# Gate order, fills from SBUF, kept weights, and final sums by accumulating transfers in a graph and expert layer

## The chip, the cores and the metric

The kernel runs on one core of one Trainium2 chip. The metric is the time that the device takes for one execution, in microseconds (us). Before the change it is 1561.77 us, the median of three runs (1561.69, 1561.77, 1563.81).

## The reference

`x` has 10000 rows of 128 values, `adj` is 10000 x 10000. First comes a graph layer, then a layer of eight experts of which each row uses the best two:

```
def _L0_gnn_ref(user_feat, item_feat, adj, W_item, b_item, W_user, b_user):
    h = item_feat @ W_item.T + b_item
    b = user_feat @ W_user.T + b_user
    return relu(adj @ h + b)
x = x + _L0_gnn_ref(layernorm(x), item_feat, adj, ...)
# experts, on xf = layernorm(x): N = 10000, D = 128, H = 256, E = 8
probs = softmax(xf @ gate_w + gate_b)
top2_vals, top2_idx = top_k(probs, 2)
cw = zeros((N, E)).at[rows, top2_idx].add(top2_vals)
for e in range(E):
    acc += cw[:, e] * (gelu(xf @ W1[e] + b1[e]) @ W2[e] + b2[e])
x = x + acc
```

All values are float32. The kernel gets that precision from TensorE by splitting a float32 operand into a rounded part ("hi") and the remainder ("lo") and adding three products.

## The kernel before

**Graph stage.** The 10000 output rows are 20 blocks of 500 (`UB`). A block runs through 26 chunks (`CH`) of 384 rows of `adj`; the counter `n` goes over all 520 (`NCH`), and `c` is the chunk within its block. For each chunk SyncE loads 750 KB into one of six buffers (`load_raw`, L295), ScalarE rounds them into `a_hi` (L743, three buffers), the vector engine makes the remainder `a_lo` (L952, two buffers), and TensorE runs nine matmuls (L497, L498, L502). `load_raw(n)` waits until the remainder of chunk n - 6 is made.

**Gate work.** While block b runs, the finished block b - 1 is taken through layer norm, gate logits, softmax, the two best experts, a prefix count and the slots of its rows. Each piece stands at a chunk number of its own, the constants `X1_AT` to `TABLE_AT`: statistics at c = 4 and 5 (`stats2`, `stats1`), then eleven small Pool instructions for the inverse deviation (`rstd`, L1315 to L1331, issued at `BN1_AT`), which `logits` (L998, `LG_AT`) and `ln2_norm` on ScalarE (L788, `LN2_AT`) wait for, Pool's `power` (L1335), `softmax`, `top`, `mask`, `prefix`, `slots`. At `SLOT_AT` Pool sends every row of the block with eight indirect transfers (L1344) to its slots in the HBM tensor `zs`, twice, once for each chosen expert.

**Expert tiles.** The first 17 blocks (`S`) are served in this sparse way, in two groups (12 and 5 blocks). After a group's last block the vector engine makes a table of tiles of 512 rows (`table`). SyncE then fills the end of each expert's region from a spare region of `zs` (`fill_ends`, eight transfers from HBM to HBM, all at `n == FILL_AT[g]`), since the last tile of an expert is not full, and after the first fill loads weights and rows of tiles 0 and 1. There are 48 tiles (`NT`), spread over the chunks that are left by `W1_AT` and the lists made from it: tile rows loaded (`load_zt`), turned (L581), two expert layers, turned back, and sent by Pool with indirect transfers (L1353) to the HBM tensor `rr`, in the original row order, the first choice to its first half and the second choice to its second.

**Dense items.** The last three blocks are done densely: 24 items (`ND`, three blocks by eight experts), one per step d after chunk 520, on all engines. In a step ScalarE does the two gelus (L857), a rounding (`dense_round`) and a weight rounding (`w_round`); the vector engine does `scale` (L1174), `dense_rest` (L1178), `w_rest` (L1135) and `comb_add`; TensorE `dense_w1`, `dense_wbc`, `dense_w2`. The gate of the last block (p = 19) runs in the same steps: logits at d = 6, softmax at d = 10. Weights are loaded and split again for each of the 24 items.

**Final sums.** For each of the 17 sparse blocks SyncE loads three 256 KB pieces (the stored rows of `out_s` and the two halves of `rr`) into SBUF, three buffers of each (`CB`), the vector engine adds them (L1187 and L1189), and SyncE stores the sum. This runs in the steps of the dense items (`COMB_AT`).

Every engine takes its instructions in the written order and waits on semaphores. No planner is used; the order is made by the constants above.

## Time and profile before

| | |
|---|---|
| median of three runs | 1561.77 us |
| the profiled execution's own time | 1562.79 us |
| its span | 1561.0 us |
| granted TensorE clock, mean | 0.979 |
| busy: matmuls, vector engine, ScalarE, Pool | 1476.0, 1278.2, 1103.5, 807.3 us |
| moved | 502.29 MB, mean 322 GB/s |

The page divides the span into 40 slices of 39 us and gives the busy tenths of each engine in them:

```profile
PE   8999999999999999999996899999999989999887
DVE  5778788788788887887885788888888978788898
ACT  4666767667677677677673778797878768787655
POOL 0114534634635544446344178776877865676420
```

TensorE is busy in nearly all of them; slice 22 (around 850 us) and the last ones are lower. A busy share says nothing on what is late, so the rows below come from waits, timelines and windows.

### The profile page before, as it was taken

How to read it: one execution, taken by the hardware profiler on the slowest of the kernel's cores; microseconds unless marked ns; L12 is line 12 of the kernel's file. 1: busy time of each engine (PE TensorE's matmuls, PEld its weight loads, DVE VectorE, ACT ScalarE, POOL GpSimd, SP SyncE). 2: the span in 40 equal slices, each digit the busy share in tenths (PEclk: the TensorE clock that was granted, in tenths of full speed). 3: DMA queues.
4: the chain of work that ended last, by engine and by line, in shares of the span. 5: the costliest groups of instructions: out<-in, count | busy, mean ns of one | idle time of the engine just before them, and what ended most of it. 6: DMA issues, size and time to landing. Idle time of an engine off the chain costs nothing.

```text
span 1561.0 us, 20673 instructions
## 1 busy us (share of the span) xinstructions
PE 1476.0 (95%) x6682; PEld 1181.8 (76%) x6682; DVE 1278.2 (82%) x1677; ACT 1103.5 (71%) x1178; POOL 807.3 (52%) x596
## 2 busy tenths in 40 slices
PE   8999999999999999999996899999999989999887
PEld 6787787787787877877875688888888877777555
DVE  5778788788788887887885788888888978788898
ACT  4666767667677677677673778797878768787655
POOL 0114534634635544446344178776877865676420
PEclk9999999999999999999998899999999999999999
DMA  9889999999999999999996998989898888786675
GB/s 356 298 315 337 351 371 345 354 365 335 369 346 340 375 343 343 382 331 355 364 331 227 348 329 320 334 331 333 322 332 326 324 306 304 273 280 226 215 237 195
DMA packets 144649, 502.29 MB, mean 322 GB/s; under 512 B 35696, under 2 KB 41792, under 8 KB 144286
## 3 DMA queue, kind: packets, MB, share of 16 engines
q1 hardware_dynamic: 127518, 479.25, 84.1%
q0 software_dynamic: 17024, 21.73, 4.1%
q8 instruction: 53, 0.87, 0.2%
q14 instruction: 54, 0.44, 0.1%
HBM read 468.77 MB, written 36.31 MB: 324 GB/s over the span
## 4 chain that ended last, share of the span: by engine, by line
PE 57%; DVE 15%; POOL 13%; issue 7%; ACT 3%; DMA 3%; SPq 2%; DVEq 0%; ACTq 0%; POOLq 0%
PE p_agg L502 16%; PE p_agg L497 14%; PE p_agg L498 14%; DVE s_a_lo L952 6%; POOL s_rs L1315 3%; POOL rr L1353 2%; POOL s_rs L1327 2%; PE p_hid L479 2%; DVE s_h_hi L1178 1%; POOL s_rs L1316 1%; ACT s_a_hi L743 1%; DMA s_raw<-adj 1%; POOL s_rs L1319 1%; PE p_agg L513 1%; PE p_hid L590 1%
## 5 line engine op out<-in xcount | busy, mean ns | idle before, releaser
L952 DVE TENSOR_TENSOR s_a_lo<-s_raw,s_a_hi 128x1500 fp32r<-128x1500 f32 x520 | 885.6, 1717 | 144.7 <-PE p_agg L502 92.4
L743 ACT ACTIVATE s_a_hi<-s_raw 128x1500 fp32r<-128x1500 f32 x520 | 751.0, 1454 | 220.2 <-PE p_agg L502 183.1
L497 PE MATMUL p_agg<-s_a_hi,s_h_hi 128*128 128x500 f32 x1560 | 635.4, 407 | 22.7 <-ACT s_a_hi L743 22.7
L498 PE MATMUL p_agg<-s_a_hi,s_h_lo 128*128 128x500 f32 x1560 | 615.1, 394 | 0.0
L502 PE MATMUL p_agg<-s_a_lo,s_h_hi 128*128 128x500 f32 x1560 | 450.8, 398 | 33.4 <-DVE s_a_lo L952 31.8
L1344 POOL DMA_INDIRECT zs<-s_rows,s_idx x136 | 225.6, 1659 | 309.2 <-DVE s_idx L1080 215.3
L502 PEld LDWEIGHTS p_agg<-s_a_lo,s_h_hi 128*128 128x128 f32 x1560 | 293.9, 191 | 115.1 <-DVE s_a_lo L952 56.6
L497 PEld LDWEIGHTS p_agg<-s_a_hi,s_h_hi 128*128 128x128 f32 x1560 | 299.4, 192 | 87.6 <-ACT s_a_hi L743 29.4
L498 PEld LDWEIGHTS p_agg<-s_a_hi,s_h_lo 128*128 128x128 f32 x1560 | 299.8, 192 | 58.1 <-issue 3.2
L1353 POOL DMA_INDIRECT rr<-s_ysb,s_dests x192 | 271.7, 1415 | 136.7 <-DVE s_ysb L1163 84.4
L1335 POOL TENSOR_TENSOR s_gt<-s_ebase,s_gt 125x32 f32<-125x32 f32 x20 | 129.9, 6495 | 48.3 <-DVE s_gt L1006 48.1
L1315 POOL TENSOR_TENSOR s_rs<-s_bn 125x8 f32<-125x8 f32 (+1 forms) x21 | 42.0, 2002 | 146.3 <-DVE s_bn L971 135.5
L1154 DVE TENSOR_TENSOR s_gl<-s_g,s_gh 128x1024 fp32r<-128x1024 f32 x48 | 58.8, 1226 | 57.1 <-ACT s_gh L833 57.1
L826 ACT ACTIVATE s_g<-p_hid,s_bias 128x512 f32<-128x512 f32 x96 | 60.5, 683 | 41.0 <-PE p_hid L592 41.0
L833 ACT ACTIVATE s_gh<-s_g 128x1024 fp32r<-128x1024 f32 x48 | 51.0, 1062 | 16.1 <-PE p_y L608 15.0
L788 ACT ACTIVATE s_rows<-p_agg,s_rs 125x128 f32<-125x128 f32 x80 | 29.9, 454 | 42.6 <-POOL s_rs L1331 42.6
L839 ACT ACTIVATE s_yt<-p_y,s_bias 128x512 f32<-128x512 f32 x48 | 32.8, 683 | 30.3 <-PE p_y L608 30.3
L590 PE MATMUL p_hid<-s_zh,s_wt 128*128 128x512 f32 (+1 forms) x106 | 43.2, 408 | 0.4 <-ACT s_g L857 0.4
L819 ACT ACTIVATE s_zh<-p_tp 128x512 fp32r<-128x512 f32 x48 | 28.0, 584 | 20.1 <-PE p_hid L592 18.1
L591 PE MATMUL p_hid<-s_zh,s_wt 128*128 128x512 f32 (+1 forms) x106 | 41.6, 392 | 0.0
L592 PE MATMUL p_hid<-s_zl,s_wt 128*128 128x512 f32 (+1 forms) x106 | 41.6, 392 | 0.0
L1135 DVE TENSOR_TENSOR s_wt<-s_wraw,s_wt 128x512 fp32r<-128x512 f32 x60 | 40.8, 680 | 0.0
(215 smaller groups left out, 1433.2 us busy)
## 6 DMA issues: line engine op xcount, KB each, us to landing
s_raw<-adj SPq DMA_DIRECT2D x520, 750.0 KB, 6.7
s_wraw<-w SPq DMA_DIRECT2D x72, 256.0 KB, 4.1
s_zt<-zs SPq DMA_DIRECT2D x48, 264.0 KB, 3.1
s_raw<-rr SPq DMA_DIRECT2D x34, 256.0 KB, 3.8
s_xtok<-x_tok SPq DMA_DIRECT2D x20, 256.0 KB, 6.8
s_xt<-x_t SPq DMA_DIRECT2D x20, 250.0 KB, 7.1
out_s<-s_x1s SPq DMA_DIRECT2D x17, 256.0 KB, 6.9
s_raw<-out_s SPq DMA_DIRECT2D x17, 256.0 KB, 3.3
```

The lines of the kernel that those rows point to most:

```text
L497: mm(o, h_hi[:, k * D:(k + 1) * D], hi, start=(k == 0), stop=False)
L498: mm(o, h_lo[:, k * D:(k + 1) * D], hi, start=False, stop=False)
L502: last = mm(o, h_hi[:, k * D:(k + 1) * D], a_lo[:, n % LOS, j * UB:(j + 1) * UB], start=False, stop=False)
L590: mm(hid[h][:, 0:n], w_hi, hi, start=True, stop=False)
L743: fn(a_hi[:, n % HIS, :], raw[:, n % RAW, :], ACT.Copy).then_inc(hi_made, 1)
L826: fn(g[:, h * T:(h + 1) * T], hid[h][:, :], ACT.Gelu, bias=bias[:, k % 4, h:h + 1])\
L952: tt(a_lo[:, n % LOS, :], raw[:, n % RAW, :], a_hi[:, n % HIS, :].bitcast(F32), ALU.subtract)\
L1154: tt(gl[:, :], g[:, :], gh[:, :].bitcast(F32), ALU.subtract).then_inc(gl_made, 1)
L1315: tt(row[0], even, odd, ALU.add)
L1335: gp.tensor_tensor(gt[0:TS, 2, :], ebase[0:TS, :], gt[0:TS, 1, :], ALU.pow).then_inc(ez_made, 1)
L1344: gp.indirect_dma_start(out=zs[:, :], out_offset=bass.IndirectOffsetOnAxis(ap=idx[0:TS, j:j + 1].bitcast(U32), axis=0), in_=rows[k][0:TS, ...
L1353: gp.indirect_dma_start(out=rr[:, :], out_offset=bass.IndirectOffsetOnAxis(ap=dests[:, k % XR, s:s + 1].bitcast(U32), axis=0), in_=yrows(k ...
```

## The change

```diff
-X1_AT, X1T_AT, BN2_AT, BN1_AT, X1S_AT, LG_AT, LN2_AT = 1, 1, 4, 5, 4, 9, 10
-TAILHI_AT, TAILLO_AT, SOFT_AT, TOP1_AT, TOP2_AT, LN1_AT = 9, 10, 15, 16, 17, 13
-PREFIX_AT, LN1T_AT, SLOT_AT, LN1C_AT = 18, 16, 20, 19
-TABLE_AT = (20, 21, 22)
+X1_AT, X1T_AT, BN2_AT, BN1_AT, X1S_AT, LG_AT, LN2_AT = 1, 1, 4, 5, 4, 11, 12
+TAILHI_AT, TAILLO_AT, SOFT_AT, TOP1_AT, TOP2_AT, LN1_AT = 9, 10, 16, 17, 18, 15
+PREFIX_AT, LN1T_AT, SLOT_AT, LN1C_AT = 19, 17, 21, 20
+TABLE_AT = (21, 22, 23)
...
-CB = 3
-FILL_AT = [(hi + 1) * CH + 5 for lo, hi in GROUPS]
-FIRST_W1 = [(hi + 1) * CH + 10 for lo, hi in GROUPS]
+CB = 12
+FILL_AT = [(hi + 1) * CH + 6 for lo, hi in GROUPS]
+FIRST_W1 = [at + E // 2 + 4 for at in FILL_AT]
...
-ZT_LOAD = [0, 0] + [max(W1_AT[k - 2] + 3, FILL_AT[k >= NTG[0]] + 1) for k in range(2, NT)]
-COMB_AT = [p + p // CB for p in range(S)]
+ZT_LOAD = [0, 0] + [max(W1_AT[k - 2] + 3, FILL_AT[k >= NTG[0]] + E // 2) for k in range(2, NT)]
+COMB_AT = [p if p < GROUPS[1][0] else p + 3 for p in range(S)]
+COMB_OUT = [6 + p if p < GROUPS[1][0] else p + 10 for p in range(S)]
...
+            def fill_end(g, e):
+                if e == 0:
+                    sp.wait_ge(scattered, 2 * 16 * SUBS * GROUPS[g][1])
+                    sp.wait_ge(tab_made, 2 * (g + 1))
+                r = sp.value_load(fillat[0:1, g, e:e + 1], min_val=0, max_val=SPARE0[g] - T)
+                sp.dma_start(zs[bass.ds(r, T), :].rearrange("(p s) w -> p (s w)", s=SUBS),
+                             fill.rearrange("p s w -> p (s w)")).then_inc(filled, 16)
...
-                    if n == FILL_AT[g_]:
-                        fill_ends(g_)
-                if n == FILL_AT[0] + 1:
+                    if 0 <= n - FILL_AT[g_] < E // 2:
+                        fill_end(g_, 2 * (n - FILL_AT[g_]))
+                        fill_end(g_, 2 * (n - FILL_AT[g_]) + 1)
+                if n == FILL_AT[0] + E // 2:
                     load_w(0)
...
-                if j + 4 < ND:
+                if j + 4 < E:
                     load_w(NT + j + 4)
...
+            def comb_add(p, k):            # on Pool
+                ...
+                pool.wait_ge(comb_loaded[p % CB], 16 * (p // CB + 1))
+                if k == 1:
+                    pool.wait_ge(comb_added[p % CB], 32 * (p // CB) + 16)
+                row = k * RANK + p * T
+                gp.dma_start(comb(p), rr[row:row + T, :].rearrange("(p s) d -> p (s d)", s=SUBS), accum_op=ALU.add)\
+                    .then_inc(comb_added[p % CB], 16)
...
-                        if k == NT - 2:
-                            power(BLOCKS - 1)
+            for first, last in ((0, GROUPS[1][0]), (GROUPS[1][0], S)):
+                for p in range(first, last + 2):
+                    if p < last:
+                        comb_add(p, 0)
+                    if p - 2 >= first:
+                        comb_add(p - 2, 1)
+                    if p == 4:
+                        power(BLOCKS - 1)
```

It has four parts. The gate pieces stand one or two chunks later. The fills are written from an SBUF tile (`fill`, in the space of the early constants) two at a time over four chunks, from `FILL_AT` on, and the first tiles' loads come after the last of them; the tiles keep their chunks. In the dense steps the eight experts' weights stay in SBUF (three sets where they were, five in the space of `h_lo`), so 8 loads and splits are left of 24; all biases come once, early, in `dbias`. And the final sums are made by 34 transfers that Pool issues and that add a piece of `rr` onto the loaded rows of `out_s` in SBUF; there are 12 buffers, the stores stand in the dense steps by `COMB_OUT`, and the power of the last block's gate stands among the adds, after the eighth. The vector engine's `comb_add` is gone.

## Rows read from the trace of the kernel before

**Rows 1.** Waits, TensorE 100 to 830, then 0 to 830, then whole: us, times, longest.
```profile
PE p_agg L502 <- DVE s_a_lo L952: 28.2, 14, 2.3
DVE s_gt L998 <- POOL s_rs L1331: 39.5, 12, 3.3
ACT s_a_hi L743 <- DMA s_raw<-adj: 36.2, 9, 17.9
```
**Rows 2.** Timeline of Pool at 720 us: start, duration, instruction, idle before.
```profile
720.87 3.24 POOL L1315 TENSOR_TENSOR s_rs<-s_bn 125x8 f32<-125x8 f32 x1 [9.24 <-DVE s_bn L971]
...
728.67 1.67 POOL L1327 TENSOR_TENSOR s_rs<-s_rs,s_consts 125x8 f32<-125x8 f32 x1
...
730.70 0.20 POOL L1331 TENSOR_TENSOR s_rs<-s_rs,s_consts 125x8 f32<-125x8 f32 x1
```
**Rows 3.** Timeline of the vector engine and TensorE at the same place.
```profile
726.05 1.76 DVE L952 TENSOR_TENSOR s_a_lo<-s_raw,s_a_hi 128x1500 fp32r<-128x1500 f32 x1 [0.32 <-PE p_agg L502]
731.01 0.19 DVE L998 TENSOR_TENSOR s_gt<-p_small,s_rs 125x32 f32<-125x32 f32 x1 [3.19 <-POOL s_rs L1331]
...
731.79 1.71 DVE L952 TENSOR_TENSOR s_a_lo<-s_raw,s_a_hi 128x1500 fp32r<-128x1500 f32 x1
...
733.55 0.94 PE L502 MATMUL p_agg<-s_a_lo,s_h_hi 128*128 128x500 f32 x3 [2.18 <-DVE s_a_lo L952]
```
**Rows 4.** Chain in order of time, 720 to 745: start, us, what.
```profile
735.28 0.42 PE p_agg L498
...
739.22 0.23 PE p_agg L497
```
**Rows 5.** Windows: stretch, its us, busy (count) by engine, clock, DMA share, GB/s.
```profile
513.00:574.00 61.00, 58.42 (x266) 47.31 (x265) 50.89 (x62) 43.20 (x39) 30.40 (x21) 1.00 0.96 354
```
**Rows 6.** First fill: SyncE's wait, its fills, TensorE's first matmul after.
```profile
SPq L380 <- DMA zs<-s_rows,s_idx: 11.6, 1, 11.6
...
842.37 10.22 SPq L381 DMA_DIRECT2D zs<-zs  x8
...
860.64 0.78 PE L497 MATMUL p_agg<-s_a_hi,s_h_hi 128*128 128x500 f32 x1 [14.88 <-ACT s_a_hi L743]
```
**Rows 7.** Timeline: turn of tile 0, and TensorE after the second fill.
```profile
871.32 0.60 PE L581 MATMUL p_tp<-s_ident,s_zt 128*128 128x128 f32 x4
...
1273.27 0.49 PE L497 MATMUL p_agg<-s_a_hi,s_h_hi 128*128 128x500 f32 x1 [3.82 <-ACT s_a_hi L743]
```
**Rows 8.** Groups by line and shape, 1451 to 1561: busy us, mean ns, idle before.
```profile
L1178 DVE TENSOR_TENSOR s_h_hi<-s_raw,s_h_hi 128x1000 fp32r<-128x1000 f32 x12 | 14.3, 1193 | 0.0
...
L1189 DVE TENSOR_TENSOR s_raw<-s_raw 128x512 f32<-128x512 f32 x17 | 11.8, 692 | 0.6
...
L1135 DVE TENSOR_TENSOR s_h_hi<-s_wraw,s_h_hi 128x512 fp32r<-128x512 f32 x12 | 8.2, 682 | 0.0
```
**Rows 9.** Timeline: the first scale of the dense items, and the last two.
```profile
1453.94 1.19 DVE L1174 TENSOR_TENSOR s_raw<-s_raw,p_agg 128x1000 f32<-128x1000 f32 x1
...
1547.63 1.20 DVE L1174 TENSOR_TENSOR s_raw<-s_raw,p_y 128x1000 f32<-128x1000 f32 x1 [0.77 <-ACT s_raw L857]
...
1551.31 1.20 DVE L1174 TENSOR_TENSOR s_g<-s_g,p_y 128x1000 f32<-128x1000 f32 x1
```
**Rows 10.** Timeline: a small Pool sum started behind an L952 at 1104.40.
```profile
1104.43 1.75 POOL L1325 TENSOR_TENSOR s_rs<-s_rs 125x8 f32<-125x8 f32 x1
```
**Rows 11.** Timeline of Pool's last instructions.
```profile
1482.74 5.46 POOL L1335 TENSOR_TENSOR s_gt<-s_ebase,s_gt 125x32 f32<-125x32 f32 x1 [9.78 <-DVE s_gt L1006]
1488.40 1.52 POOL L1353 DMA_INDIRECT rr<-s_ysb,s_dests  x1 [0.20 <-issue]
1490.23 0.96 POOL L1353 DMA_INDIRECT rr<-s_ysb,s_dests  x1 [0.30 <-issue]
```
**Rows 12.** DMA issues with KB and median us to landing; chain, 1380 to 1450.
```profile
s_raw<-rr SPq DMA_DIRECT2D x34, 256.0 KB, 3.8
...
1401.41 5.79 DMA rr<-s_ysb,s_dests
```

More of the change, by code:

```diff
@@ L140, in build @@
         dests = sb("dests", [P, XR, SUBS], I32)
-        early = sb("early", [P, 3 * D])
+        early = sb("early", [P, SUBS * W])
         wi, ones, bbs = early[:, 0:D], early[:, D:2 * D], early[0:4, 2 * D:3 * D]
@@ L159, in build @@
         ints = sb("ints", [1, NTHR + NTG[0] + E * E])
-        fill = ysb[:, :, :].rearrange("p a n -> p (a n)")[:, 0:SUBS * W].rearrange("p (s w) -> p s w", w=W)
+        fill = early[:, :].rearrange("p (s w) -> p s w", w=W)
         bn = sb("bn", [P, 2 * SUBS, 6])
@@ L225, in build @@
         sent = [sem("sent0"), sem("sent1")]
-        rr_zeroed, comb_mid, comb_made = sem("rr_zeroed"), sem("comb_mid"), sem("comb_made")
+        rr_zeroed = sem("rr_zeroed")
+        comb_added = [sem(f"comb_added{i}") for i in range(CB)]
         comb_loaded = [sem(f"comb_loaded{i}") for i in range(CB)]
@@ L265, in wpart, with comb, parts_made @@
         def wpart(o, lo):
-            i = (o - NT) % 6
-            if o >= NT and i >= 3:
-                w0 = 12 * UB + (i - 3) * 4 * HID + lo * 2 * HID
-                return h_hi[:, w0:w0 + 2 * HID]
+            e = (o - NT) % E
+            if o >= NT and e >= 3:
+                w0 = (e - 3) * 4 * HID + lo * 2 * HID
+                return h_lo[:, w0:w0 + 2 * HID]
+            if o >= NT:
+                return wt[:, e, lo, :]
             return wt[:, o % 3, lo, :]
-        def wpart_before(o):
-            return o - 3 if o < NT + 3 else o - 6
         def yrows(k):
             return ysb[:, k % 2, :]
-        def comb(p, i):
-            c0 = 2 * UB + p % CB * 3 * T + i * T
+        def comb(p):
+            c0 = 2 * UB + p % CB * T
             return flat[:, c0:c0 + T]
-        def tiles_to(o):
-            return min(o, NT)
+        def parts_made(o):
+            return min(o, NT + E - 1) + 1
         block = ctx.enter_context(nc.Block())
@@ L446, in _ @@
             load_w(NT + 3)
-            for j in range(ND + 4):
+            for j in range(ND + 5):
                 for p in range(S):
-                    if COMB_AT[p] == j - 3:
+                    if COMB_OUT[p] == j:
                         comb_store(p)
@@ L804, in w_round @@
             def w_round(o):
-                act.wait_ge(w_loaded[o % 2], 32 * (o // 2 + 1))
-                before = wpart_before(o)
-                if NT + 3 <= o < NT + 6:
+                late = max(o - NT + 2, 0) // 2
+                act.wait_ge(w_loaded[o % 2], 32 * (o // 2 + 1) - 16 * late)
+                if o >= NT + 3:
                     act.wait_ge(chunk_used, NCH)
-                elif before >= 0:
-                    act.wait_ge(w2_done, before + 1)
+                elif o >= 3:
+                    act.wait_ge(w2_done, o - 2)
                 fn(wpart(o, 0), wraw[:, o % 2, :], ACT.Copy).then_inc(w_hi, 1)
@@ L932, in _ @@
                     dense_round(d - 1)
-                if d >= 0 and d + 2 < ND:
+                if 0 <= d and d + 2 < E:
                     w_round(NT + d + 2)
@@ L1272, in _ @@
                     dense_rest(d - 1)
-                if d >= 0 and d + 2 < ND:
+                if 0 <= d and d + 2 < E:
                     w_rest(NT + d + 2)
-                for p in range(S):
-                    if COMB_AT[p] == d - 2:
-                        comb_add(p)
                 if d >= E + 3 and (d - 3) % E == 0:
@@ L1335, in power @@
                 gp.tensor_tensor(gt[0:TS, 2, :], ebase[0:TS, :], gt[0:TS, 1, :], ALU.pow).then_inc(ez_made, 1)
+            def comb_add(p, k):
+                if k == 0 and p == 0:
+                    pool.wait_ge(rr_zeroed, 16 * 3)
+                if k == 0 and (p == 0 or p == GROUPS[1][0]):
+                    for i in range(2):
+                        pool.wait_ge(sent[i], 16 * SUBS * tiles_of(i, NT if p else NTG[0]))
+                pool.wait_ge(comb_loaded[p % CB], 16 * (p // CB + 1))
[4 more added lines that the diff above has]
+                    .then_inc(comb_added[p % CB], 16)
             def scatter(p):
@@ L1363, in _ @@
             gp.memset(rows[1][:, :, :], 0.0).then_inc(sets, 1)
-            gp.memset(ysb[:, :, :], 0.0).then_inc(sets, 1)
-            pool.wait_ge(sets, 5)
+            pool.wait_ge(sets, 4)
             pool.wait_ge(late_loaded, 16 * NL)
-            gp.tensor_scalar(fill[:, :, D + 1], dest0[:, :], float(DUMP + 2 * T), None, ALU.add).then_inc(spare_set, 1)
             for i in range(2):
@@ L1383, in _ @@
                         scatter(p)
+                if n == 2 * CH:
+                    pool.wait_ge(h_prod, CH + 1)
+                    pool.wait_ge(gsum_done, 1)
+                    pool.wait_ge(bb_split, 1)
+                    gp.memset(fill, 0.0).then_inc(fill_set, 1)
+                    pool.wait_ge(fill_set, 1)
+                    gp.tensor_scalar(fill[:, :, D + 1], dest0[:, :], float(DUMP + 2 * T), None, ALU.add)\
+                        .then_inc(fill_set, 1)
                 for k in range(NT):
```

67 lines of the change are left out of this document (25 added, 42 removed).

## The prediction

> **What bounds the kernel now.** I read the table of waits first, then one block of the graph stage in the timeline, then the two fills, then the dense stage. In the first half TensorE is the limit: between 100 and 830 us its matmuls stood still only 28.2 us, all of it behind the remainder chunks of L952 [rows 1]. The block at 720 us shows where this comes from. The eleven small Pool instructions of `rstd` begin at 720.87 and the last one at 730.70; the vector engine reaches `logits` (L998) at 727.8 and idles 3.19 us for them [rows 2, 3]. The next remainder starts at 731.79 in place of 728.10 (one chunk of 2.05 us behind 726.05), 3.69 us late, and the matmuls lose 2.18 us: so TensorE has 1.5 us of slack there. After the idle time its matmuls come 0.42 us apart (granted clock low), then 0.23 us again [rows 4]. Ten of them at the lower level cost 2.0 us. The waits count 12 such blocks; one stretch of a block (513 to 574) shows full clock, so not each of them pays the 2.0 us [rows 1, 5].
>
> The second loss is the fill at 842 us. SyncE waited 11.6 us for the last scatter, then issued eight HBM-to-HBM fills in 10.22 us, and raw chunks stood behind all that; TensorE idled 14.88 us, restarted at the low clock, and reached the first expert tile's turn (L581) only at 871.32 [rows 6, 7]. The second fill cost 3.82 us of idle and some slow matmuls [rows 7].
>
> The third is the end. From 1452 us on, one dense item of the vector engine is scale 1.19, remainder 1.19, weight remainder 0.68 and, for 17 items, two sums of 0.69 [rows 8]; from the first scale at 1453.94 to the last at 1551.31 that is 97.4 us for 23 steps, 4.23 each. The step from 1547.63 to 1551.31 has no weight remainder, and its two sums fit beside ScalarE: 3.68 us, set by the ring scale, remainder, gelu [rows 9].
>
> **The change part by part.** All is summed against the profiled execution, 1562.79 us, of which the span is 1561.0.
>
> *Gate order.* `logits` moves two chunks later (9 to 11), `ln2_norm` to 12, the rest of the gate mostly by one. Two chunks are 4.1 us, more than the 3.2 us wait, so on paper the wait goes. The rows speak against the whole of it: a small Pool sum takes 0.20 us, but 1.75 us when an L952 started just before it [rows 2, 10]. At 727.9 us six Pool instructions are left. With the vector engine idle they take 3.0 us. In the new order it runs two more remainders and `tail_rest` in that time, gaps of 0.3 us at most, so Pool gets through perhaps two of the six; the power (1.67) and the two behind it come after 732.1, where `logits` now stands waiting. I get `rs` at 734.4, the next remainder at 735.2, 3.1 us late against 3.69 before: TensorE waits 1.5 us and not 2.2. Over 12 blocks 0.65 x 12 = 7.8 us. An idle time of 1.5 us may no longer drop the clock each time; I take four drops fewer, 4 x 2.0 = 8.0 us. Sum 15.8. Ends: no drop saved and 0.3 us a block, 4 us; the stall gone with its slow matmuls, 12 x 4.2 = 50 us. I stay near the low end because a wait of 3.0 us of Pool's own work can't shrink while its engine neighbour is busy. Raw chunks needed faster have room: ScalarE waited for raw data in nine places only, 36.2 us in all, 17.9 of it in one at the first fill [rows 1]. Behind the later waits of softmax and `slots` stand five chunks in place of six for a Pool power of 5.5 us or more [rows 11]; five are 10 us or more, so I cost this at 0.
>
> *Fills.* Scatter and fill both move one chunk, so the 11.6 us wait stays. Then two fills (2.6 us at 1.28 each, from SBUF) come before a raw chunk, where eight (10.2) did. The ring holds one chunk more, so TensorE runs dry at 848, and raw 345 lands near 851.5: idle 5 us in place of 14.9. But the loads of tile 0 now stand behind all fills and four raw chunks, near 861, and TensorE is in order: it waits for that tile at chunk 345 until about 864.6, and is slow again. The turn of tile 0 comes 6.7 us earlier less 2 us of clock: gain 4.5 us (0 if a wait in the fills piles up, 12 if neither stands). For the second fill the raw chunk is in time; gain 4 of the 5.6 us lost (0 to 5.6). Sum 8.5.
>
> *Kept weights.* 16 of 24 weight loads, roundings (ScalarE) and remainders (0.68 us on the vector engine) go, and the biases come in one early load of many tiny rows behind which nothing was late: 0.
>
> *Sums by accumulating transfers.* All 34 sums leave the vector engine. With the weights gone a step is 3.68 us, bound by the ring: 3.32 + 22 x 3.68 = 84.3, plus 2.0 for the extra work at steps 11 and 14, against 97.4: 11.1 us. The new cost is in Pool's queue. `power` for the last block (5.46 us, now begun at 1482.74 right after `logits`, before the last send [rows 11]) moves behind the last send and eight accumulating transfers. An indirect send costs Pool 0.96 to 1.52 and 0.30 between [rows 11]; I take 1.45 for an add. The last send ends at 1478; three adds, a wait of 2 us for the first to land, five adds: 1491.5; power done at 1497.2. Softmax at step 10 would run at 1493.3, and behind it in the vector queue stand the scale and remainder of step 11, for which ScalarE and TensorE wait: 3.9 us, of which 3.6 are not covered, and a 0.5 us clock loss. Net gain 7.0. If an add costs 1.25, 9; if 2.7, softmax waits 12 us and the stage loses 1.
>
> The other 26 adds last until 1535; refilling a buffer before the second group costs 5, landing and store 9: 1549, five before the main path's end at 1554. The trace has no accumulating transfer. The nearest rows: a plain 256 KB load of `rr` lands in 3.8 us, an indirect send in 5.79 [rows 12]. By the order of issue two adds are in flight, so one per 1.45 us (Pool's issue) at best and one per 2.9 us if each takes 5.8: 34 x 2.9 = 99 us. I take the issue-bound value, since a plain load lands sooner than that. Stores wait on SyncE in order, and later loads of `out_s` stand behind them; the four items between hide that while adds land within about 6 us.
>
> Pool's sends take 0.96 to 1.52 us beside a busy vector engine [rows 11]. The Trainium skill ("SBUF — State Buffer", the box on the vector engine blocking DMA) warns that transfers issued by GpSimd starve while that engine holds the shared port, and gives some 3.1 us in place of 0.62 for one; by it 34 adds would take 105 us and the tail would end after that of before. The trace does not agree for these sends; no run shows it for an accumulating one.
>
> **Sum.** 15.8 + 8.5 + 0 + 7.0 = 31.3; 1562.8 - 31.3 = 1531.5; the median of the runs shown is 1.0 below the profiled one: 1531.
>
> **Rivals.** *A, the gate wait is gone wholly*: the two chunks suffice and 50 us come back in place of 15.8. For it: 4.1 > 3.2 and no idle, no clock loss. Against it: [rows 10]. Time 1497. *B, the gate stall keeps its clock falls and the fills merely move*: 4 + 4 + 7 = 15; 1547. For it: 1.5 us of idle is much still. *C, the adds become the bound, the slower side*: Pool's accumulating transfers land in 5.8 us or more, one per 2.9 us; they begin at 1478, so the last is done at 1577, with the refill, landing and store 1590, 29 us past the old end, and 24.3 us of gate and fills don't cover it: 1566. It decides from 2.7 us per add on, where the tail's loss equals those 24. For it: each reads and writes SBUF besides reading HBM; against it the 3.8 us landing [rows 12]. *D, the change hits a wait that I don't see in the expert stage* (power one chunk closer to softmax behind Pool's sends), 48 tiles losing 0.5 us each: 1555.
>
> **How the numbers follow.** Forecast 0.45, A 0.15, B 0.2, C 0.12, D 0.08. 1531 is the likeliest. Its own range is 1518 to 1545 (gate 8 to 24, fills 3 to 13, tail -1 to 9). The range over cases goes down into A and up to just short of C: 1502 to 1561. A measurement of this kernel tells 0.2% (3 us). Faster: forecast, A, B and most of D, 0.85; slower: C less its mild half, and some of D, 0.11; same 0.04.
>
> **What would show it.** Right: at `logits` in a first-half block the vector engine idles 2.2 to 2.5 us and L502 waits about 1.5; a Pool sum of 1.7 us stands between 728 and 732 of such a block; TensorE's idle at the first fill is two pieces of 5 and 8 us, the second ended by the `zt` load; dense steps of 3.68 us, one of 7 to 8 at softmax. Wrong: no idle before L998 at all (A); Pool's adds 2.5 us or more apart with the last store far behind the last dense output (C); waits on `ez` in the expert stage (D).

## The result and the profile after

The changed kernel takes 1535.07 us (median of 4 runs, 1534.02 to 1538.60) against 1562.79 for the kernel before (4 runs, 1561.69 to 1564.05), ratio 0.9829 with a 95% interval of 0.9817 to 0.9841: 27.7 us faster. The prediction was 1531, range 1502 to 1561. The profiled execution took 1538.60, span 1536.8, so the traces differ by 24.2 us only, and the changed kernel's other runs lie about 3.5 below its profiled one.

Where the 24.2 us come from is read by following one instruction through both traces. The remainder L952 runs once per chunk, 520 times; the start of number n in the trace of before less its start in the trace of after is what has been gained by then:

```
chunk number          4    28   104   312   338   346   366   370   390   468   480   519   end
gained by then, us  -3.8  -3.7  -1.2   4.3   4.7  17.6  15.0   9.1   8.5   8.8  15.9  16.0  24.2
```

So 3.8 us are lost at the very start, 8.6 gained in the graph stage, 10.2 at the first fill (338 to 366), 6.5 lost right behind it, 7.1 gained at the second fill (468 to 480), and 8.2 in the dense stage and the end.

*The gate.* The wait table of the changed kernel, 100 to 830 us (us in total, times, longest), answers to [rows 1]:

```profile
DVE s_gt L998 <- POOL s_rs L1320: 26.3, 12, 2.2
PE p_agg L501 <- DVE s_a_lo L952: 23.4, 22, 1.9
```

The vector engine idles 2.2 us for `rstd` where it idled 3.2, and TensorE's wait falls by only 4.8 us in all. At `logits` it falls from 2.2 or 2.3 to 1.6 in eleven of the twelve blocks (1.9 in one), 7.7 us together. But smaller waits have come behind it: 0.13 us where ScalarE is late after `ln2_norm`, and 0.3 us eight chunks later, beside the vector engine's `top`. The same block in the timelines, which answers to [rows 2, 3]:

```profile
717.04 3.23 POOL L1304 TENSOR_TENSOR s_rs<-s_bn 125x8 f32<-125x8 f32 x1 [7.64 <-DVE s_bn L971]
...
726.80 3.15 POOL L1316 TENSOR_TENSOR s_rs<-s_rs,s_consts 125x8 f32<-125x8 f32 x1
...
730.30 0.20 POOL L1320 TENSOR_TENSOR s_rs<-s_rs,s_consts 125x8 f32<-125x8 f32 x1
...
730.60 0.19 DVE L998 TENSOR_TENSOR s_gt<-p_small,s_rs 125x32 f32<-125x32 f32 x1 [2.20 <-POOL s_rs L1320]
...
734.08 3.35 DVE L952 TENSOR_TENSOR s_a_lo<-s_raw,s_a_hi 128x1500 fp32r<-128x1500 f32 x2 [0.98 <-ACT s_a_hi L742]
...
733.16 0.94 PE L501 MATMUL p_agg<-s_a_lo,s_h_hi 128*128 128x500 f32 x3 [1.58 <-DVE s_a_lo L952]
```

Pool's eleven instructions take 13.46 us from 717.04 to their end (13.2 to 13.5 in all twelve blocks); in [rows 2] they took 10.03. There the last six of them started after 727.9, when the vector engine was idle already; here only the last two did. What a block of 26 chunks costs is in the windows (stretch, its us, busy (count) of TensorE, its weight loads, vector engine, ScalarE and Pool, granted clock, DMA share, GB/s). First two blocks of the kernel before, one at full clock and one not:

```profile
507.20:567.60 60.40, 58.09 (x265) 47.09 (x264) 50.68 (x63) 42.62 (x39) 29.96 (x20) 1.00 0.95 349
628.40:689.40 61.00, 58.72 (x262) 48.04 (x262) 50.72 (x63) 42.66 (x38) 30.61 (x20) 0.97 0.97 362
```

and two of the changed one:

```profile
624.80:684.90 60.10, 57.98 (x264) 46.69 (x263) 50.68 (x63) 42.55 (x38) 33.57 (x20) 1.00 0.97 361
684.90:745.60 60.70, 58.74 (x260) 47.47 (x258) 50.81 (x62) 42.67 (x38) 33.22 (x20) 0.97 0.96 358
```

A fall of the clock costs a block 0.6 us, not 2.0, and the shorter stall saves it 0.3, not 0.65. Before, 11 of the 12 stretches from chunk 18 to 330 show 0.97 or 0.98; after, 4 do.

*The start.* SyncE and TensorE (the first line is the new load of all biases):

```profile
9.32 0.39 SPq L398 DMA_DIRECT2D s_dbias<-b  x1
9.75 3.77 SPq L399 DMA_DIRECT2D s_yt<-tri  x1
...
19.75 0.43 PE L475 MATMUL p_hid<-s_bbp,s_bselr 4*128 4x384 f32 x1 [1.63 <-DMA s_g<-feat_t]
```

The small load behind the biases held SyncE 3.77 us (0.33 in the kernel before), and raw and feature chunks stood behind it.

*The fills*, answering to [rows 6, 7]. In the kernel before, TensorE had a second idle time behind the 14.88 us, and on SyncE the loads of tiles 0 and 1 stood between the first raw chunk behind the fills and the second:

```profile
852.64 0.57 SPq L295 DMA_DIRECT2D s_raw<-adj  x1
...
858.81 0.91 SPq L295 DMA_DIRECT2D s_raw<-adj  x2
...
867.74 0.79 PE L497 MATMUL p_agg<-s_a_hi,s_h_hi 128*128 128x500 f32 x1 [3.23 <-ACT s_a_hi L743]
```

In the changed kernel: SyncE's first two fills, TensorE's two idle times, and the turn of tile 0.

```profile
838.73 1.49 SPq L379 DMA_DIRECT2D zs<-s_early  x2
...
848.36 0.79 PE L496 MATMUL p_agg<-s_a_hi,s_h_hi 128*128 128x500 f32 x1 [5.71 <-ACT s_a_hi L742]
...
865.19 0.78 PE L496 MATMUL p_agg<-s_a_hi,s_h_hi 128*128 128x500 f32 x1 [3.36 <-ACT s_a_hi L742]
...
868.65 0.60 PE L580 MATMUL p_tp<-s_ident,s_zt 128*128 128x128 f32 x4
```

The idle times fall from 18.1 us together to 9.1. Then comes a wait that the kernel before did not have. Pool issues the scatters of block 12 ahead of the send of tile 0, and tile 2's result has to wait for that send:

```profile
896.85 1.27 POOL L1346 DMA_INDIRECT zs<-s_rows,s_idx  x1 [22.27 <-DVE s_idx L1080]
...
917.70 0.99 POOL L1355 DMA_INDIRECT rr<-s_ysb,s_dests  x1 [0.30 <-issue]
...
927.93 0.69 DVE L1161 TENSOR_TENSOR s_ysb<-p_y,s_probs 128x512 f32<-128x512 f32 x1 [5.80 <-DMA rr<-s_ysb,s_dests]
...
930.91 1.62 PE L501 MATMUL p_agg<-s_a_lo,s_h_hi 128*128 128x500 f32 x3 [4.00 <-DVE s_a_lo L952]
```

At the second fill TensorE no longer idles at all ([rows 7] had 3.82).

*The end*, answering to [rows 9, 11]: first and last scale, softmax without a wait, Pool's power, the last vector result, the last accumulating transfer.

```profile
1437.72 1.19 DVE L1172 TENSOR_TENSOR s_raw<-s_raw,p_agg 128x1000 f32<-128x1000 f32 x1
...
1477.11 0.18 DVE L1013 TENSOR_REDUCE s_col<-s_gt 125x4 f32<-125x32 f32 x1
...
1522.53 1.20 DVE L1172 TENSOR_TENSOR s_g<-s_g,p_y 128x1000 f32<-128x1000 f32 x1 [1.38 <-ACT s_g L857]
...
1527.91 0.68 DVE L1181 TENSOR_TENSOR s_xt<-p_y,s_xt 128x500 f32<-128x500 f32 x1 [1.88 <-PE p_y L664]
...
1470.09 6.27 POOL L1324 TENSOR_TENSOR s_gt<-s_ebase,s_gt 125x32 f32<-125x32 f32 x1
...
1528.82 0.86 POOL L1336 DMA_DIRECT2D s_raw<-rr  x1 [2.53 <-DMA s_raw<-rr]
```

23 steps take 84.81 us (97.4 in [rows 9]); but for the first (3.15) and two of 3.95 and 4.03 they are 3.67 to 3.73 each. Yet the last accumulating transfer is issued after the last vector result, and the span ends 8.2 us behind that result (1536.8 less 1528.6), where it ended 2.5 behind it in the kernel before (last result 1557.76 to 1558.44). The adds on the page (busy us, mean ns, idle before; then KB and us to landing), and Pool's waits for them in the wait table of 1440 to 1537:

```profile
L1336 POOL DMA_DIRECT2D s_raw<-rr x34 | 31.0, 1134 | 32.8 <-DMA s_raw<-out_s 16.7
...
s_raw<-rr POOLq DMA_DIRECT2D x34, 256.0 KB, 6.7
```

```profile
POOL s_raw L1336 <- DMA s_raw<-out_s: 16.7, 5, 6.5
POOL s_raw L1336 <- DMA s_raw<-rr: 15.5, 9, 2.6
```

### The profile page after: what moved, and what is told of

Read it like the earlier page. It is cut to its first block, busy times and chain, and to the rows that moved or that the text cites. A ratio compares the mean times of both kernels' runs of the same rounds, so it can differ in the third digit from the quotient of the medians.

```text
span 1536.8 us, 20551 instructions
## 1 busy us (share of the span) xinstructions
PE 1469.6 (96%) x6682; PEld 1172.5 (76%) x6682; DVE 1248.4 (81%) x1627; ACT 1095.3 (71%) x1162; POOL 885.7 (58%) x630
## 4 chain that ended last, share of the span: by engine, by line
PE 49%; DVE 15%; POOL 14%; issue 8%; ACT 7%; DMA 5%; SPq 2%; POOLq 0%; ACTq 0%; DVEq 0%
PE p_agg L501 13%; PE p_agg L496 11%; PE p_agg L497 11%; DVE s_a_lo L952 9%; ACT s_a_hi L742 4%; POOL s_rs L1316 3%; DMA s_raw<-rr 3%; POOL s_rs L1304 2%; POOL zs L1346 2%; POOL s_rs L1312 1%; POOL s_rs L1305 1%; PE p_hid L478 1%; PE p_hid L589 1%; PE p_hid L591 1%; PE p_hid L590 1%
## 5 line engine op out<-in xcount | busy, mean ns | idle before, releaser
L952 DVE TENSOR_TENSOR s_a_lo<-s_raw,s_a_hi 128x1500 fp32r<-128x1500 f32 x520 | 885.8, 1718 | 139.4 <-PE p_agg L501 84.4
L496 PE MATMUL p_agg<-s_a_hi,s_h_hi 128*128 128x500 f32 x1560 | 630.6, 404 | 10.2 <-ACT s_a_hi L742 10.1
L1346 POOL DMA_INDIRECT zs<-s_rows,s_idx x136 | 231.9, 1705 | 306.3 <-DVE s_idx L1080 211.8
L501 PEld LDWEIGHTS p_agg<-s_a_lo,s_h_hi 128*128 128x128 f32 x1560 | 290.2, 190 | 120.2 <-DVE s_a_lo L952 63.3
L497 PEld LDWEIGHTS p_agg<-s_a_hi,s_h_lo 128*128 128x128 f32 x1560 | 297.3, 191 | 57.9 <-issue 3.2
L1355 POOL DMA_INDIRECT rr<-s_ysb,s_dests x192 | 277.4, 1445 | 102.7 <-issue 53.1
L1316 POOL TENSOR_TENSOR s_rs<-s_rs,s_consts 125x8 f32<-125x8 f32 (+1 forms) x21 | 55.7, 2655 | 1.6
L1336 POOL DMA_DIRECT2D s_raw<-rr x34 | 31.0, 1134 | 32.8 <-DMA s_raw<-out_s 16.7
L746 ACT ACTIVATE s_h_hi<-p_hid 128x384 fp32r<-128x384 f32 x26 | 12.8, 491 | 41.2 <-PE p_hid L478 41.2
L589 PE MATMUL p_hid<-s_zh,s_wt 128*128 128x512 f32 (+1 forms) x102 | 41.7, 409 | 0.4 <-ACT s_g L857 0.4
```

The lines of the kernel that those rows point to most:

```text
L496: mm(o, h_hi[:, k * D:(k + 1) * D], hi, start=(k == 0), stop=False)
L497: mm(o, h_lo[:, k * D:(k + 1) * D], hi, start=False, stop=False)
L501: last = mm(o, h_hi[:, k * D:(k + 1) * D], a_lo[:, n % LOS, j * UB:(j + 1) * UB], start=False, stop=False)
L952: tt(a_lo[:, n % LOS, :], raw[:, n % RAW, :], a_hi[:, n % HIS, :].bitcast(F32), ALU.subtract)\
L1316: tt(row[1], row[5], mhalf, ALU.pow).then_inc(rs_step, 1)
L1346: gp.indirect_dma_start(out=zs[:, :], out_offset=bass.IndirectOffsetOnAxis(ap=idx[0:TS, j:j + 1].bitcast(U32), axis=0), in_=rows[k][0:TS, ...
```

## The experiments

All are the changed kernel with the edit shown, but for the fourth; times are medians of 4 runs, ratios to the kernel before on the same chip, with 95% intervals. They ran on two chips, where the kernel before took 1561.74 to 1563.74 us, so a difference to the changed kernel's 1535.07 of 2 us or less says little. The "gained by" numbers are made as in the table above.

**Bias load later.**
```
-                    sp.dma_start(dbias[:, :, :], b12.rearrange("e p n -> p e n")).then_inc(late_loaded, 16)
...
+                if n == 40:
+                    sp.dma_start(dbias[:, :, :], b12.rearrange("e p n -> p e n")).then_inc(dbias_loaded, 16)
```


> The changed kernel with one edit: the one load of all biases (dbias) is issued at chunk 40 of the graph stage and not among the first small loads. Theory 'the bias load is paid': in the changed kernel's trace SyncE's next load (tri) takes 3.77 us behind it where it took 0.33, raw and feature chunks stand behind that, and the remainder of chunk 4 is 3.8 us late against the kernel before. Then that time comes back: the remainder of chunk 4 at 24.1 to 24.5 us and not 27.9, and about 3.8 us of the total, 1531.3. Rival 'the start has slack, what is lost there comes back in the first block': the total stays at 1535 within 1 us, and the lag against before is gone by chunk 52 anyway (it was 2.8 there, and 1.2 at chunk 104). A third: at chunk 40 the same many tiny rows hold up SyncE for 3.4 us again, and raw chunks with it; then less than 3.8 comes back, though six raw chunks are in the ring.

1536.67 us, ratio 0.9828 (0.9804 to 0.9852): no gain. In its trace the hold is gone and with it the lag at chunk 4, 0.5 us and not 3.8:

```profile
8.30 0.33 SPq L399 DMA_DIRECT2D s_yt<-tri  x1
```

The hold is the bias load's: it stands in all seven other traces with the early load (2.86 to 3.59 us) and in none without. At chunk 40 the next load is held too, as the third theory has it (its issue takes 1.38 us in place of 0.33), but no engine waits for it. The rival that the first block takes the lag back falls: this trace is 3.3 us ahead of the changed kernel's at chunk 4 and still 2.9 at chunk 519. What the hold costs is not settled all the same: the lags at chunk 4 in the seven other traces with the early load are 0.4 to 4.4 us (2.4 in the mean of all eight), and one without the hold was 2.0 late too (0.3 in the mean of six). The total shows no gain, and its interval is nearly 4 us wide to either side.

**Send first.**
```
-                    if c == SLOT_AT and p < S:
+                    if c == SLOT_AT and p < S and p != GROUPS[1][0]:
                         scatter(p)
...
                         send(k)
+                        if k == 0:
+                            scatter(GROUPS[1][0])
```


> The changed kernel with one edit: on Pool the eight scatters of block 12 (the first ones after the first fill) are issued behind the send of expert tile 0 and not ahead of it. Theory 'sends are queued behind the scatters': in the changed kernel's trace the vector engine waits 5.80 us at 922 for the send of tile 0, whose four transfers were issued at 917.7 behind scatters that began at 896.85; the matmuls L501 wait 4.00 us for it and run slowly after. Then the wait goes, TensorE has no idle of 4 us between 905 and 940, and 6 to 6.5 us come back: 1529. Rival 'Pool is simply full there': eight scatters and two sends take 22 us whatever their order, so the wait moves to the next tile (tile 3 waits for the send of tile 1) and less than 2 us come back: 1533 to 1535.

1530.83 us, ratio 0.9805 (0.9779 to 0.9832). Pool now sends first:

```profile
894.56 1.24 POOL L1355 DMA_INDIRECT rr<-s_ysb,s_dests  x1 [23.61 <-DVE s_ysb L1161]
...
901.03 1.21 POOL L1346 DMA_INDIRECT zs<-s_rows,s_idx  x1 [0.30 <-issue]
```

and from 905 to 935 no engine waits for a send. The gain at chunk 366 is still there at 370 (18.5 and 18.5; 15.0 and 9.1 in the changed kernel). The wait came from the order on Pool, and it cost 6 us at that place. The medians differ by 4.2, but the intervals of the two ratios overlap, so it is the trace that shows it. The rival, that Pool is full in either order, falls.

**Sums ahead.**
```
-COMB_AT = [p if p < GROUPS[1][0] else p + 3 for p in range(S)]
-COMB_OUT = [6 + p if p < GROUPS[1][0] else p + 10 for p in range(S)]
+COMB_AT = [p // 2 if p < CB else p - 5 for p in range(S)]
+COMB_OUT = [6 + p if p < GROUPS[1][0] else p + 8 for p in range(S)]
...
-                    if p - 2 >= first:
-                        comb_add(p - 2, 1)
+                    if p - 3 >= first:
+                        comb_add(p - 3, 1)
```


> The changed kernel with the order of the final sums changed: the loads of out_s into the twelve buffers are issued two per step from the start of the dense stage, and the second accumulating transfer of a piece comes three pieces behind its first, not two. Theory 'the adds end last': in the changed kernel's trace the last vector result is ready at 1528.6 and the end is at 1536.8, 8.2 us later, where it was 3.3 us after the last result in the kernel before; Pool waits 16.7 us for loads of out_s and 15.5 us for its own first transfers. Then the adds end before the last result and 4 to 5 us come back: 1530.5. Rival 'the adds are bound by transfers': each needs its 6.7 us landing and the queue lets few be in flight, so Pool's waits move and the end stays within 1.5 us: 1535. A second rival: more adds at once slow the last expert sends or dense steps (3.68 us a step): then steps grow.

1530.88 us, ratio 0.9793 (0.9774 to 0.9811). From chunk 519 to the end it gains 13.6 us over the kernel before, the changed one 8.2. The last add now stands ahead of the last vector result, and the span (1530.0) ends 2.8 us behind that (timeline, and Pool's wait in the wait table of 1440 to 1531):

```profile
1520.50 0.86 POOL L1336 DMA_DIRECT2D s_raw<-rr  x1 [3.05 <-DMA s_raw<-rr]
...
1526.56 0.68 DVE L1181 TENSOR_TENSOR s_xt<-p_y,s_xt 128x500 f32<-128x500 f32 x1 [1.87 <-PE p_y L664]
```

```profile
POOL s_raw L1336 <- DMA s_raw<-rr: 25.0, 11, 6.4
```

The steps stay at 3.68. The waits for loads are gone, those for Pool's own transfers grew from 15.5 to 25.0: the adds are bound by their landing now (8.7 us in the median, 6.7 in the changed kernel), but end in time.

**Gate order alone**, on the kernel before (first fill and first tile one chunk later with the scatter).
```
-X1_AT, X1T_AT, BN2_AT, BN1_AT, X1S_AT, LG_AT, LN2_AT = 1, 1, 4, 5, 4, 9, 10
...
+X1_AT, X1T_AT, BN2_AT, BN1_AT, X1S_AT, LG_AT, LN2_AT = 1, 1, 4, 5, 4, 11, 12
...
+FILL_AT = [(hi + 1) * CH + 6 for lo, hi in GROUPS]
+FIRST_W1 = [(hi + 1) * CH + 11 for lo, hi in GROUPS]
```


> The kernel before with the gate order of the changed one alone (logits 11, ln2_norm 12, softmax 16 and the rest by one or two; first fill and first expert tile one chunk later with the scatter). The prediction gave this part 15.8 us: 1547. Reading the two traces block by block gives less: a block of 26 chunks takes 61.2 us where the clock falls and 60.4 where not in the kernel before, 60.7 and 60.1 in the changed one, so 12 x 0.35 for the stall plus about 7 falls fewer x 0.8 = 9.5 us: 1554. If the stall had gone with its slow matmuls (rival A) it would be 1512.

1551.75 us, ratio 0.9936 (0.992 to 0.9953): 10.0 us, where the prediction has 15.8 and the reading of the traces 9.5. In its trace 8.5 us of that come between chunk 4 and 338, as in the changed kernel, and four of the twelve blocks show the low clock. Its second fill still idles:

```profile
1264.69 0.78 PE L497 MATMUL p_agg<-s_a_hi,s_h_hi 128*128 128x500 f32 x1 [3.89 <-ACT s_a_hi L743]
```

**Logits at 13.**
```
-X1_AT, X1T_AT, BN2_AT, BN1_AT, X1S_AT, LG_AT, LN2_AT = 1, 1, 4, 5, 4, 11, 12
...
+X1_AT, X1T_AT, BN2_AT, BN1_AT, X1S_AT, LG_AT, LN2_AT = 1, 1, 4, 5, 4, 13, 14
+TAILHI_AT, TAILLO_AT, SOFT_AT, TOP1_AT, TOP2_AT, LN1_AT = 9, 10, 17, 18, 19, 16
+PREFIX_AT, LN1T_AT, SLOT_AT, LN1C_AT = 20, 18, 22, 21
...
+FILL_AT = [(hi + 1) * CH + 7 for lo, hi in GROUPS]
```


> The changed kernel with logits two chunks later again (13, ln2_norm 14, softmax 17, slots 22, first fill and first tile one chunk later). Theory 'Pool's small instructions end only when the vector engine pauses': each remainder of L952 holds up one of them, so two more chunks (4.1 us) let about two more of the eleven through, the idle time before logits falls from 2.2 by about 1.0 as from 9 to 11 (3.19 to 2.20), and TensorE waits about 0.6 us a block where it waited 1.9: 12 to 14 us, 1522. Rival 'it is only time': 4.1 us more is over the 2.2 us wait, no idle at all before logits, the block at full clock takes 58.2 us (TensorE's busy time) and 22 to 26 us come back: 1511. Rival 'softmax now stands too close behind the power': four chunks are 8.2 us against a power of 6.8; then a wait on Pool stands before softmax and nothing comes back: 1535.

1517.06 us, ratio 0.9714 (0.9698 to 0.973): 18 us below the changed kernel, between the first theory's 1522 and the rival's 1511. The trace decides for the rival. Pool and the vector engine in the timeline, TensorE's waits from 100 to 790 us, and the window of one block:

```profile
691.85 3.24 POOL L1304 TENSOR_TENSOR s_rs<-s_bn 125x8 f32<-125x8 f32 x1 [5.59 <-DVE s_bn L971]
...
705.12 0.20 POOL L1320 TENSOR_TENSOR s_rs<-s_rs,s_consts 125x8 f32<-125x8 f32 x1
...
706.82 0.18 DVE L998 TENSOR_TENSOR s_gt<-p_small,s_rs 125x32 f32<-125x32 f32 x1
```

```profile
PE p_agg L501 <- DVE s_a_lo L952: 5.4, 18, 0.5
```

```profile
659.00:717.00 58.00, 57.33 (x262) 46.81 (x261) 50.74 (x63) 42.54 (x39) 33.19 (x20) 1.00 0.99 368
```

In this block Pool's chain again takes 13.47 us, with the vector engine at work to its end. Its length is no constant: over the twelve blocks it is 9.2 to 15.1 us here. But logits, now 15.0 us behind the chain's start, finds `rs` ready in all of them (its idle time is 0.2 us at most), the block takes 58 us at full clock, and between chunk 4 and 338 34.6 us are gained over the kernel before. The softmax rival costs nothing in this stage.

**Logits at 15.**
```
+X1_AT, X1T_AT, BN2_AT, BN1_AT, X1S_AT, LG_AT, LN2_AT = 1, 1, 4, 5, 4, 15, 16
+TAILHI_AT, TAILLO_AT, SOFT_AT, TOP1_AT, TOP2_AT, LN1_AT = 9, 10, 19, 20, 21, 18
+PREFIX_AT, LN1T_AT, SLOT_AT, LN1C_AT = 22, 20, 24, 22
+TABLE_AT = (24, 25, 26)
...
+FILL_AT = [(hi + 1) * CH + 9 for lo, hi in GROUPS]
```


> The same at 15 (ln2_norm 16, softmax 19, slots 24, first fill and first tile three chunks later than in the changed kernel). By the first theory the idle time before logits is 0.2 us or none now, TensorE waits nothing for the rest of the gate and a block takes 58.2 to 58.6 us; by the second it is as at 13 in the graph stage. Both fills and the expert stage come three chunks later, which leaves 6 us less to the expert tiles: in the graph stage 20 to 24 us come back, of the total 16 to 24: 1511 to 1519.

1538.10 us, ratio 0.9843 (0.9826 to 0.9859), a miss. The graph stage is as at 13 (57.8 to 57.9 us a block from the fifth on), 29.5 us gained at chunk 338. The expert stage loses it: 18.6 at 442 and 9.2 at 519. (The profiled execution was the longest of the four, 8.2 us above the median.) Starting the expert tiles three chunks later costs far more than 6 us. Among the longer waits are some for Pool's sends: the vector engine idles 7.4 us for one at 916 and 3.1 at 1024. Which of the waits the total pays for was not tested.

**Vector sums.** Three loads and two sums of the vector engine for each piece, `power` ahead of the last send, as in the kernel before; kept weights stay.
```
+                tt(comb(p, 1), comb(p, 1), comb(p, 2), ALU.add).then_inc(comb_mid, 1)
...
+                tt(comb(p, 0), comb(p, 0), comb(p, 1), ALU.add).then_inc(comb_made, 1)
...
-                gp.dma_start(comb(p), rr[row:row + T, :].rearrange("(p s) d -> p (s d)", s=SUBS), accum_op=ALU.add)\
-                    .then_inc(comb_added[p % CB], 16)
```


> The changed kernel with the final sums as before (three loads and two sums of the vector engine for each piece, power before the last send), kept weights and all else left as changed. Theory 'the steps come from the kept weights, the transfers only cost': the kernel before already took 3.68 us for the one step that had two sums and no weight remainder, so the steps stay at 3.68 to 3.8, the last vector result comes by 1530 and the end 3.3 us behind it and not 8.2: 1531 to 1533, faster than the changed kernel. Rival 'the transfers bring the steps down': with 1.2 us of sums back on the vector engine 17 steps take 4.2 and the end comes 8 us later: 1543.

1538.31 us, ratio 0.9848 (0.9831 to 0.9864), 3.2 above the changed kernel, which the two intervals just fail to separate. Both theories hold half. The end (1539.4) comes 2.7 us behind the last vector result (1536.66), much as in the kernel before (2.5), but that result comes 8.1 us later than in the changed kernel. Steps with sums alone do take 3.68; most of those that have a weight remainder or gate work beside the sums take 4.1 to 5.4, such as this one of 4.15 between two starts of the remainder:

```profile
1445.06 1.19 DVE L1180 TENSOR_TENSOR s_h_hi<-s_g,s_h_hi 128x1000 fp32r<-128x1000 f32 x1
...
1449.21 1.21 DVE L1180 TENSOR_TENSOR s_h_hi<-s_raw,s_h_hi 128x1000 fp32r<-128x1000 f32 x1
```

So the transfers give 8 us up to the last result and take 5.5 back behind it. This kernel also prices the kept weights: its dense stage differs from that of before in them (and in the biases that are loaded early) alone, and from chunk 519 to the end it gains 5.0 us over the kernel before. Against the kernel with the sums ahead the vector sums cost 7.4 us.

**Fills from HBM, fills in a row.**
```
# the first kernel
-                             fill.rearrange("p s w -> p (s w)")).then_inc(filled, 16)
+                             zs[SPARE0[g]:SPARE0[g] + T, :].rearrange("(p s) w -> p (s w)", s=SUBS)).then_inc(filled, 16)
# the second kernel
-                    if 0 <= n - FILL_AT[g_] < E // 2:
-                        fill_end(g_, 2 * (n - FILL_AT[g_]))
-                        fill_end(g_, 2 * (n - FILL_AT[g_]) + 1)
+                    if n == FILL_AT[g_]:
+                        for e in range(E):
+                            fill_end(g_, e)
```


> The changed kernel with the end-of-list fills read again from the spare rows in HBM, but still two before each of four raw chunks. In the changed kernel two fills from SBUF take SyncE 1.46 us and in the kernel before eight from HBM took 10.2 (2.6 for two). Theory 'the order gives the gain, the source adds a little': 1.1 us more before each raw chunk, 4.4 us more before the first expert tile's loads; the first fill's two idle times (5.71 and 3.36) grow by 1 to 4 us together, the second fill stays without an idle time: 1.5 to 5 us slower, 1537 to 1540. Rival 'the source gives the gain' (the HBM fills also slow the raw chunks that land beside them): the second fill gets back its 3.8 us of idle time and slow matmuls, the first up to 6: 1543 or more.

> The changed kernel with all eight fills from SBUF issued in a row ahead of the first raw chunk (as the kernel before did from HBM). 8 x 0.73 = 5.9 us of SyncE before that chunk where it was 1.5, so the first idle time of TensorE at the first fill grows from 5.7 to about 10, while the raw chunks behind come without fills between them and the second idle time of 3.4 goes; the first expert tile is loaded as early or earlier. Theory 'the fills' SyncE time is what the first stretch pays, in whatever order': the total stays within 2 us, 1534 to 1537. Rival 'the order gives the gain': 4 to 8 us slower, the second fill with an idle time again: 1540.

1538.40 us (ratio 0.9841, 0.9819 to 0.9863) and 1536.93 (0.9832, 0.9813 to 0.985): neither can be told from the changed kernel. SyncE and TensorE with the eight in a row:

```profile
837.43 8.76 SPq L379 DMA_DIRECT2D zs<-s_early  x8
...
852.69 0.78 PE L496 MATMUL p_agg<-s_a_hi,s_h_hi 128*128 128x500 f32 x1 [11.32 <-ACT s_a_hi L742]
```

The idle time is one of 11.3 us (TensorE's next is 0.58, at 864.33) and not two of 9.1 together, but from chunk 338 to 366 this kernel gains 9.9 us and the changed one 10.2. (Eight fills took 8.76 us and not 5.9: the 0.73 of the expectation is half the span of a pair, but the next fill starts 1.1 us behind the one before it, in a pair as in a row.) With the fills from HBM the idle times are 12.2 us together, within the 1 to 4 us more that were expected, and the gain is 9.1. Both kernels keep the gain at the second fill (7.2 and 7.4 us from chunk 468 to 480), where the gate order alone did not have it.

So neither the source nor the spreading is needed alone. What is left is the third part of the edit: the first tiles' loads stand four chunks behind the start of the fills and not one, and the first layer of the first tile eight and not five. For the first fill SyncE's queue speaks for it: in the kernel before, two raw chunks are 6.2 us apart there, with the tiles' loads between them (852.64 and 858.81 above), and in the kernel with eight fills in a row four raw chunks come ahead of those loads. But that part was not undone alone, and no kernel has both the HBM source and the row with it, so that either of the two may do where the other is missing: it is argued, not shown.

**The three edits together, and with logits at 12 and at 13.**

> The three edits together: bias load at chunk 40, scatters of block 12 behind the first send, loads of out_s ahead and adds three pieces apart. If the three costs lie on one path one after the other they add up: 3.8 + 6.3 + 4.9 = 15 us off the changed kernel's 1535, so 1520. If one hides another (the start's lag is caught up in the first fill's wait, say), 1524 or more.

> The three edits (bias load at chunk 40, block 12's scatters behind the first send, sums ahead and three apart) with logits at 12 and ln2_norm at 13, all else of the gate as in the changed kernel. Pool's eleven instructions take 13.46 us from their start in the changed kernel and also with logits at 13; at 11 the vector engine idled 2.20 for them. One chunk (2.04) more leaves about 0.2: nearly all of the stall goes, a block takes 58.2 to 58.6 us in place of 60.3, and since slots and fills are not moved nothing is lost in the fills: 1524 - 12 x 1.9 = 1501, perhaps 1499 to 1505. Rival 'Pool shares time with the vector engine': if the chain stretches when the vector engine runs one more remainder beside it, half of the idle time stays: 1512.

> The three edits with the gate of logits at 13 (all that follows one chunk later, the first fill and tile too). Alone, logits at 13 took the changed kernel from 1535 to 1517 (its first fill idles 8.41 and 3.00 us where it was 5.71 and 3.36), the three edits took it to 1524.3. If they add up: 1506. The expert stage of this gate lost some 6 us against the other by the time it began the dense stage; if that was the queue of scatters and sends, the swap gives it back: 1503.

1524.25 us (ratio 0.9755, 0.9737 to 0.9774), 1514.33 (0.9689, 0.967 to 0.9708) and 1513.12 (0.9682, 0.9666 to 0.9699). The three edits bring 10.8 us of the 15 expected; the two that showed alone bring 8.4 by their own medians, so nothing speaks against their adding up. Logits at 12 leaves an idle time of 0.6 us before logits in each block (6.7 us in 12), not 0.2, and of 23 us 10 come back: the graph stage gains 26.8 us from chunk 4 to 338 (the three edits alone 9.0), and some 7 are lost again around chunk 381. At 13 the graph stage gains 35.2, and the same 7 are lost at the same place, about what is missing to the 1506. In both, softmax now waits there 5.36 us for Pool's power, which stands behind the sends of two tiles; neither the three edits with logits at 11 nor logits at 13 without them have this wait. Why 13 is hardly better than 12, though its graph stage gains 8.4 us more: it gains 2.5 us less at the first fill and loses 5.8 between chunk 480 and 519, where at 12 nothing is lost; the longest wait of that stretch is again for a send. The timeline at 13:

```profile
940.53 0.19 DVE L1015 TENSOR_REDUCE s_col<-s_gt 125x4 f32<-125x32 f32 x1 [5.36 <-POOL s_gt L1326]
...
944.54 1.62 PE L503 MATMUL p_agg<-s_a_lo,s_h_hi 128*128 128x500 f32 x3 [5.63 <-DVE s_a_lo L954]
...
1350.72 0.69 DVE L1163 TENSOR_TENSOR s_ysb<-p_y,s_probs 128x512 f32<-128x512 f32 x1 [4.45 <-DMA rr<-s_ysb,s_dests]
```

The first is the wait that the third theory on logits at 13 named, in the other stage. Both beat the changed kernel by 21 to 22 us.

## Why the prediction was right, and where it was not

The total was right to 4 us, and in part by luck: the traces differ by 24.2 us where 31.3 were summed up. The gate was put 6 to 7 us too high and the start's 3.8 us were not seen, while fills and dense stage came out higher than forecast. Term by term:

```
term                      predicted     measured
gate order                     15.8     10.0 alone; 8.6 in the trace
  shorter stall           7.8 (0.65)    7.7 at logits, of it 3.6 kept (0.3 a block)
  fewer low clocks       8.0 (4 x 2.0)  4 to 6 (7 x 0.6 to 0.8)
first fill                      4.5     10.2, then -6.5 by the order on Pool
second fill                     4       7.1
kept weights, bias load         0       -3.8 at the start
final sums                      7.0     8.2: 5.0 for the kept weights, 3.2 for the transfers
```

*Gate order.* The idle time before logits (2.2 to 2.5 predicted, 2.20 found), TensorE's wait (1.5; 1.58) and the length of Pool's chain (13.5 from 720.87 to 734.4; 13.46) were right, and so was choosing the low end. Two sizes were off. A low clock was priced from ten slow matmuls, 2.0 us, where whole blocks of the kernel before give 0.6 to 0.8 (61.0 to 61.2 us against 60.4). And the smaller waits behind `ln2_norm` and at `top`, which take back about half of what the wait at logits gives, were not seen. The reason given ("a wait of 3.0 us of Pool's own work can't shrink while its engine neighbour is busy") holds only up to the chain's full length: beside a busy vector engine the eleven instructions take 13.2 to 13.5 us with logits at 11 and 12, and 9.2 to 15.1 at 13. Rival A's mechanism was right, its place wrong. At 11 logits is reached 11.4 us behind the chain's start, at 12 13.0, at 13 15.0, and only the last leaves no idle time.

*Fills.* The two idle times were forecast as 5 and 8 us, the second ended by the load of tile 0. Found were 5.71 and 3.36, the second ended by a raw chunk: tile 0's place had moved four chunks back, so TensorE reached it only at 868.65, with its data there. The step that failed is the one that left tile 0 at chunk 345. The account of the change says the same ("the tiles keep their chunks"), and it is not so: `FIRST_W1` goes from 10 to 14 chunks behind the start of its block, so the first turn goes from chunk 345 to 349. The prediction also set its 5 and 8 us against 14.9, and left out that the kernel before idles 3.23 us more at 867.74. The same move put the send of tile 0 behind the scatters of block 12, which the prediction did not look for: it is rival D's kind of wait (an unseen one in the expert stage), 6 us once, not 0.5 for each of 48 tiles. The two errors nearly cancelled: 10.2 less 6.5 is 3.7, against 4.5.

*Kept weights.* Costed at nothing. The early load held SyncE 3.77 us; what the total pays for it stays open. The edit's gain in the dense steps, 5.0 us by the kernel with vector sums, was booked under the sums.

*Final sums.* The steps of 3.68 were right. Softmax did not wait (3.6 us predicted), since Pool issued half of the accumulating transfers in 0.86 to 0.90 us (1.13 in the mean) and not 1.45: power began 8.8 us behind the last send (1461.3 to 1470.1) and not 13.5, and was done 0.7 us before softmax's turn. On the other side the adds end behind the dense path and not five before it, 5 us lost: Pool waited 16.7 us for loads of `out_s` that stand behind stores on SyncE, which the prediction named and took to be hidden ("the four items between hide that"). Rival C's adds as the bound came true in its mild form, 5.4 us by the experiment with the sums ahead.

The figure of some 3.1 us that the prediction took from the Trainium skill ("SBUF — State Buffer", section "A bandwidth-pool intuition that's wrong") stands there for a transfer issued by GpSimd beside a `tensor_copy` of the vector engine. The Trainium skill says on the same page (section "Who interferes with whom") that `tensor_tensor` did not stall such transfers, and the vector engine's large instructions in the dense steps are `tensor_tensor`. The trace agrees with that sentence: five accumulating transfers were issued in 4.43 us among dense steps. No run here has the case of the 3.1 us.

## What to carry to other kernels

Take a helper chain's length beside a neighbour that never pauses, not from the trace where the neighbour waits for it, and put its consumer that far behind its start: two chunks short (logits at 11) the graph stage gained 8.5 to 9.9 us, one short 26.8, none short 34.6 to 35.2. Then look at the next stage: with logits at 13 and the three edits, two waits there took some 13 us back. When a stage is moved by some chunks, list again the order of every queue that serves two stages: here one scatter slid ahead of one send. A small clock drop is priced from whole stretches at either level, not from the slow instructions in it.
